# Gate matmuls in pairs on 64-row tiles, squares side by side, and their sum ahead of gates 0 and 1 on VectorE

## What is computed

```python
x = x + window_attention(_ln_c(x))        # 8x8 windows, 4 heads of 16, relative bias, projection
t = _to_tokens(x)                         # 65,536 tokens of 64 channels
u = _ln_t(t)                              # over a token's 64 channels
probs = softmax(u @ router_w + router_b)  # 8 experts
top_p, top_i = top_k(probs, 2); top_p /= sum(top_p)
t = t + sum_k top_p[k] * (u @ expert_w[top_i[k]] + expert_b[top_i[k]])
```

## Time and profile before

| | |
|---|---|
| median of 3 runs | 1270.95 us |
| lowest, highest | 1270.83, 1271.89 us |
| profiled execution, its own time | 1268.81 us |
| its span, first to last instruction | 1267.0 us |
| granted TensorE clock, mean | 0.983 |
| TensorE matmuls busy | 1192.4 us, 94% |
| GpSimd busy | 1081.7 us, 85% |
| VectorE busy | 1053.9 us, 83% |
| ScalarE busy | 920.4 us, 73% |

### The profile page before, as it was taken

One profiled execution on the slowest core, in us unless ns is written; L12 is line 12 of the kernel. 1 busy time (PEld: TensorE's weight loads), 2 busy tenths in 40 slices (PEclk: granted clock), 3 DMA queues, 4 the chain that ended last, 5 costly groups with the idle time before them and its releaser, 6 DMA issues.

```text
span 1267.0 us, 47630 instructions
## 1 busy us (share of the span) xinstructions
PE 1192.4 (94%) x19840; PEld 729.4 (58%) x19840; DVE 1053.9 (83%) x2247; ACT 920.4 (73%) x1743; POOL 1081.7 (85%) x925
## 2 busy tenths in 40 slices
PE   4579999999999999999999999999999999999986
PEld 3456666655565666656566666655556565666531
DVE  6458898888888889898888888988888888888874
ACT  6368778867777887877677888777767776777742
POOL 6368999989888999999988899998988888888753
PEclk9599999999999999999999999999999999999998
DMA  7012333322223233322222333332222222222221
GB/s 203 5 38 66 92 94 86 81 61 71 55 60 81 77 90 94 91 59 61 70 55 62 95 88 86 88 87 55 58 65 66 53 65 65 63 56 66 64 70 42
DMA packets 95622, 91.43 MB, mean 72 GB/s; under 512 B 26928, under 2 KB 62384, under 8 KB 95408
## 3 DMA queue, kind: packets, MB, share of 16 engines
q1 hardware_dynamic: 95408, 88.37, 27.6%
HBM read 35.90 MB, written 17.83 MB: 42 GB/s over the span
## 4 chain that ended last, share of the span: by engine, by line
PE 67%; DVE 10%; POOL 7%; DMA 7%; issue 5%; ACT 5%; SPq 0%; DVEq 0%; POOLq 0%; ACTq 0%
PE bank_y L530 16%; PE bank_s L410 8%; PE bank_t L425 8%; PE bank_s L384 6%; PE bank_o L464 4%; PE bank_g L518 4%; DMA r_b<-recip_rows 4%; PE bank_o L438 4%; PE bank_p L454 4%; PE bank_p L518 3%; DVE t_g L992 3%; DMA recip_rows<-r_out 2%; PE bank_t L394 2%; PE bank_y L502 2%; DVE prob L880 2%
## 5 line engine op out<-in xcount | busy, mean ns | idle before, releaser
L1142 POOL TENSOR_TENSOR t_g<-t_t,g_copy 128x512 f32<-128x512 f32 x192 | 245.6, 1292 | 72.0 <-ACT g_copy L712 70.8
L530 PE MATMUL bank_y<-t_g,w_exp 128*64 128x512 f32 x1024 | 268.9, 616 | 6.7 <-DVE t_g L992 4.7
L1120 POOL TENSOR_TENSOR prob<-prob,mx 128x512 f32<-128x512 f32 x256 | 261.8, 1045 | 14.7 <-DVE mx L887 14.5
L675 ACT ACTIVATE prob<-prob 128x512 f32<-128x512 f32 x256 | 159.4, 623 | 128.6 <-POOL prob L1120 128.6
L992 DVE TENSOR_TENSOR t_g<-t_t,bank_p 128x512 f32<-128x512 f32 x256 | 174.2, 680 | 9.2 <-PE bank_p L518 7.3
L880 DVE TENSOR_TENSOR prob<-bank_s,rel 128x1024 f32<-128x1024 f32 x128 | 156.3, 1221 | 28.4 <-PE bank_s L410 23.7
L425 PE MATMUL bank_t<-idn,prob 128*128 128x128 f32 x1024 | 163.6, 283 | 5.5 <-ACT v_bd L670 5.0
L679 ACT ACTIVATE prob_t<-bank_t 128x512 f32<-128x512 f32 x256 | 152.5, 596 | 21.3 <-PE bank_t L425 21.2
L712 ACT ACTIVATE g_copy<-bank_g 128x512 f32<-128x512 f32 x192 | 113.8, 593 | 74.1 <-PE bank_g L518 73.9
L425 PEld LDWEIGHTS bank_t<-idn,prob 128*128 128x128 f32 x1024 | 112.8, 141 | 79.2 <-issue 65.9
L887 DVE TENSOR_REDUCE mx<-prob 128x16 f32<-128x1024 f32 x128 | 155.4, 1214 | 2.2
(11 more groups left out here) (122 smaller groups left out, 2345.1 us busy)
## 6 DMA issues: line engine op xcount, KB each, us to landing
t_t<-t_rout SPq DMA_DIRECT2D x256, 128.0 KB, 2.4
x_in<-in_x SPq DMA_DIRECT2D x68, 256.0 KB, 3.3
r_b<-recip_rows SPq DMA_DIRECT2D x64, 256.0 KB
out_y<-y_out SPq DMA_DIRECT2D x128, 128.0 KB, 2.6
r_in<-sum_b SPq DMA_DIRECT2D x64, 16.0 KB
recip_rows<-r_out SPq DMA_DIRECT2D x64, 16.0 KB, 1.7
t_g<-in_sel SPq DMA_DIRECT2D x1, 512.0 KB, 3.6
rel<-in_relb SPq DMA_DIRECT2D x1, 256.0 KB, 2.9
```

The source lines that it names most:

```text
L530: mm(B_Y[C * a:C * a + C, :], w_exp[:, pair, :], t_g[:, (2 * pair + a) % TG, :], start=False, stop=(pair == MIXES // 2 - 1), skip_group_ch ...
L675: A(prob[:, i], prob[:, i], ACT.Exp).then_inc(p_ready.sem, 1)
L1120: G.tensor_tensor(sc, sc, mx[:, i, :].unsqueeze(2).broadcast_to([P, 2 * HEADS, NTOK]), ALU.subtract).then_inc(s_shifted.sem, 1)
L1142: G.tensor_tensor(t_g[:, u % TG, :], t_t[:, p, u % 2, :], g_copy[:, n, :], ALU.mult).then_inc(tg_pool.sem, 1)
```

## The change

The gates' parts go to other groups of `g3`, so that the first four groups (rows 0 to 63) hold all three parts for even gate matmuls, and the last four (rows 64 to 127) for odd ones. Each gate matmul then uses its 64 rows alone. Gate matmul 2 goes behind the turned logits, next to 3, and 5 goes from behind the fourth turn of probabilities to ahead of it, next to 6. Gate matmuls 4 and 7 stay where they are. The bias matmul still uses all 128 rows, with its parts in another order. `x_sq` is laid out with the eight planes of a column side by side; the squares' write steps over 32 bytes, the sum's read is contiguous. The sum is issued ahead of products 0 and 1.

```diff
--- before.py
+++ after.py
@@ -52,8 +52,9 @@
 SQUARES, PLANES, SCALES = range(3)
 CHUNK = 32
 PARTS = 3
-GATE_PARTS = (0, 0, 0, 1, 1, 1, 2, 2)
-BIAS_PARTS = (0, 1, 2, 0, 1, 2, 0, 1)
+GATE_PARTS = (0, 1, 2, 0, 1, 2, 0, 1)
+BIAS_PARTS = (0, 0, 0, 1, 1, 1, 2, 2)
+SEL_PARTS = ((0, 1, 2), (4, 5, 6))
 STAGES = ("project", "attend", "output", "route", "mix")
 LN_C_EPS, LN_T_EPS = 1e-6, 1e-5
 
@@ -110,7 +111,7 @@
 
         x_in = sb("x_in", [P, RING, 4, W])
         xt = sb("xt", [P, 2 * C, H])
-        x_sq = sb("x_sq", [P, 2, 4, H])
+        x_sq = sb("x_sq", [P, H, 2 * 4])
         plane_sum = sb("plane_sum", [P, 4, H])
         sums2 = sb("sums2", [P, H, GROUPS // 2])
         st = sb("st", [P, 5, H])
@@ -152,7 +153,7 @@
         g_copy = sb("g_copy", [P, len(ON_POOL), BANK])
         y_out = sb("y_out", [P, 4, W])
 
-        FIRST_SQ = (x_sq, prob[:, 0:2].rearrange("p i h n k -> p (i h n k)").rearrange("p (m c h) -> p m c h", m=2, c=4))
+        FIRST_SQ = (x_sq, prob[:, 0:2].rearrange("p i h n k -> p (i h n k)").rearrange("p (h x) -> p h x", x=2 * 4))
         B_S = ctx.enter_context(nc.psum_tensor("bank_s", [P, 2, BANK], F32))
         B_T, B_O, B_E, B_P, B_G, B_Y = (
             ctx.enter_context(nc.psum_tensor(f"bank_{n}", [P, BANK], F32)) for n in "toepgy")
@@ -515,7 +516,8 @@
                     pe.wait_ge(g_copied.sem, g_copied.at(g, ON_POOL.index(u - 2) + 1))
                 elif u:
                     pe.wait_ge(tg_dve.sem, tg_dve.at(g, ON_DVE.index(u - 2) + 1))
-                mm(B_GATE[u % 2][:, :], gate_sel16[:, u, :], g_t[:, :], start=True, stop=True
+                rows = slice(C * (u % 2), C * (u % 2) + C)
+                mm(B_GATE[u % 2][:, :], gate_sel16[rows, u, :], g_t[rows, :], start=True, stop=True
                    ).then_inc(gate_done[u % 2].sem, 1)
 
             def experts(g, pair):
@@ -561,11 +563,10 @@
                     logits(j - 2)
                 if attending and work.take:
                     turn_probs(j, 1, work)
-                if mixing:
-                    gates(j - 3, 2)
                 if routing_on:
                     turn_logits(j - 2)
                 if mixing:
+                    gates(j - 3, 2)
                     gates(j - 3, 3)
                 if projecting:
                     project(j + 1, QUERIES)
@@ -581,12 +582,10 @@
                     take(work.batch, *work.take, 1, j)
                 if mixing:
                     experts(j - 3, 1)
-                if mixing:
                     gates(j - 3, 6)
+                    gates(j - 3, 5)
                 if attending:
                     turn_probs(j, 3, work)
-                if mixing:
-                    gates(j - 3, 5)
                 if outputting:
                     project_out(j - 1)
                 if projecting:
@@ -625,7 +624,8 @@
                 act.wait_ge(xt_ready.sem, xt_ready.at(n, 2 * r + m + 1))
                 act.wait_ge(sq_sums.sem, sq_sums.at(batch, max(t * 2 + r - (batch == 0), 0)))
                 act.sem_inc(passed, 1)
-                A(dst[:, m], xt[:, bass.ds(plane + (2 * r + m) * 4, 4), :], ACT.Square).then_inc(sq_ready.sem, 1)
+                A(dst[:, :, 4 * m:4 * m + 4].rearrange("p h c -> p c h"), xt[:, bass.ds(plane + (2 * r + m) * 4, 4), :],
+                  ACT.Square).then_inc(sq_ready.sem, 1)
 
             def first_take(batch, t, r):
                 for m in range(2):
@@ -817,7 +817,7 @@
                 pair = bass.ds(t * 2 + r, 1)
                 dve.wait_ge(sq_ready.sem, sq_ready.at(n, 2 * r + 2))
                 V.tensor_reduce(sums2[:, :, pair].rearrange("p h o -> p (h o)"),
-                                src[:, :, :, :].rearrange("p m c h -> p h (m c)"), AX.X,
+                                src[:, :, :], AX.X,
                                 ALU.add).then_inc(sq_sums.sem, 1)
 
             def first_sums(batch, t, r):
@@ -976,13 +976,13 @@
                     elif step == 15:
                         V.tensor_tensor(gates, hot, over_experts(share), ALU.mult).then_inc(route.sem, 1)
                     elif step == 16:
-                        V.tensor_copy(g3[:, :, 0:3, :], thrice(by_pair[0], 3)).then_inc(route.sem, 1)
+                        V.tensor_copy(g3[:, :, 0::3, :], thrice(by_pair[0], 3)).then_inc(route.sem, 1)
                     elif step == 17:
                         V.tensor_tensor(by_pair[1], by_pair[0], g3[:, :, 0, :], ALU.subtract).then_inc(route.sem, 1)
                     elif step == 18:
-                        V.tensor_copy(g3[:, :, 3:6, :], thrice(by_pair[1], 3)).then_inc(route.sem, 1)
+                        V.tensor_copy(g3[:, :, 1::3, :], thrice(by_pair[1], 3)).then_inc(route.sem, 1)
                     elif step == 19:
-                        V.tensor_tensor(g3[:, :, 6:8, :], thrice(by_pair[1], 2), thrice(g3[:, :, 3, :], 2), ALU.subtract).then_inc(route.sem, 1)
+                        V.tensor_tensor(g3[:, :, 2::3, :], thrice(by_pair[1], 2), thrice(g3[:, :, 1, :], 2), ALU.subtract).then_inc(route.sem, 1)
 
             def gate(g, p, u):
                 dve.wait_ge(gate_done[u % 2].sem, gate_done[u % 2].at(g, u // 2 + 1))
@@ -1011,11 +1011,11 @@
                     total_planes(work.batch)
                 if work.step == SCALES:
                     turn_root(work.batch)
+                if work.sums:
+                    sum_squares(work.batch, *work.sums)
                 if mixing:
                     gate(j - 3, 1 - p, 0)
                     gate(j - 3, 1 - p, 1)
-                if work.sums:
-                    sum_squares(work.batch, *work.sums)
                 if routing_on:
                     routing(j - 2, 1, 8)
                 if mixing:
@@ -1220,7 +1220,7 @@
     for g in range(2):
         bexp[:, g, :, g, :] = a["eb"]
         for e in range(EXPERTS):
-            sel[[0, 3, 6], g, e, e // 2 * 2 + g, e % 2, :] = 1.0
+            sel[list(SEL_PARTS[g]), g, e, e // 2 * 2 + g, e % 2, :] = 1.0
     kmask = np.zeros((2, HEADS, DH, 2), f)
     kbias = np.zeros((2, HEADS, DH, 2), f)
     for h in range(HEADS):
```

## The result

Five runs of each on one chip: **1280.54 us** for the changed kernel (1278.73 to 1282.67), 1270.95 for the one before (1270.2 to 1272.45). Ratio **1.0074**, 95% interval 1.006 to 1.0089: slower, by 9.6 us. The profiled execution took 1280.54 us, its span is 1278.8 (1267.0 before), its mean granted clock 0.973 (0.983).

The account below looks back on a forecast made before the run. Slots were taken as a front part tied to ScalarE and VectorE and a rear part of pure TensorE. Slot terms summed to +5.6 us on 1268.8, so 1274.4, plus 2.1 to the median: 1276.5 us, range 1256 to 1283.

Parts of the forecast that it names:

- the forecast case: Whole kernel: slot terms total +5.6 us, giving 1276.5 us; chance 0.52, its own range 1272 to 1283.
- Pairs overlap in full: Paired 64-row gate matmuls on TensorE: both run together and cost one 0.21 us; bounds 0 to 0.21 saved per pair.
- A change of shape costs 0.095: TensorE, between matmuls of different tile shape: 0.095 us each, five more a slot, 0.48 in all; bounds 0 and 0.10.
- Ordinary slots, +0.20: Slots without a take: each 0.20 us longer, so +5.0 over 25 ordinary and +1.8 over 9 with statistics.
- The -0.07 of the pair 6/5: Gates 6 and 5 with the turn between, up to the output's projection: from 0.97 to 0.90 us, saving 0.07.
- Take slots, 0: 21 slots with take and sums: gate and pair terms and the removed 0.11 us wait of experts 1 total 0.
- Sums alone, -0.51: 3 slots with sums but no take: +0.20 less the 0.71 us wait of experts 1, -1.5 us in all.
- The squares' write, taken as 0: ScalarE's stepped square write costs 0, idle time being behind both squares; up to +4.6 us in the first phase.
- the bound of 0.38 each: Upper bound for a stepped square write of 512 numbers on ScalarE: 0.38 us, from VectorE's 0.76 for 1024.
- rival 3: Every pair counts in full on TensorE: 3 x 0.21 x 64 = 41 us saved, 1230 us; chance 0.02.
- changes of rows alone: Rival 1: TensorE tile changes in rows alone are nearly free, -14.8 us together, 1256 us; chance 0.27.
- the pairs don't fail to overlap: Denies rival 2: pairs of gate matmuls do not overlap, +19 us on top, 1295 us; chance 0.06.

Follow-up runs that it names:

- the experiment: Changed kernel with gate matmuls 4 and 7 on all 128 rows, the three pairs left on 64: 1270.88 us, ratio 1.0 to the kernel before.
- the sums alone: Kernel before with only the new x_sq layout, stepped square write and sum ahead of products 0 and 1: 1273.43 us, ratio 1.0023.
- the gates alone: Changed kernel with the squares' layout and the sum's place as before, only the gates' part kept: 1279.99 us, ratio 1.0076 to the kernel before.

## Why the prediction was right, and where it was not

The sign and the forecast case held: the mechanism of the slots, 0.10 us for each change of shape against pairs that save little where they stand, is what the runs show. The size was 5.6 us forecast and 9.6 measured, within the range.

That it came this near is partly luck. All 5.6 us were forecast for the slots. The 61 slots with a forecast of their own became 4.8 longer, but only since misses cancel: 3.4 less than forecast in the ordinary and the statistics slots, 1.5 more with take and sums, 0.3 more with a take alone, 0.9 more with sums alone. Another 3.4 us ahead of the first mix and 3.6 at the end were not in the sum at all.

- **Pairs overlap in full.** Starts 0 to 0.05 us apart, as forecast, from the experts' and scores' float32 rows. With the same rows they come 0.23 apart.
- **A change of shape costs 0.095.** Held. The changed slot shows +0.10 ahead of the queries' projection, +0.09 at gate 4, +0.11 at gate 7; 0.21 for two in the experiment. No load stands ahead of gate 0: its load starts at 1162.42 and its matmul at 1162.43. The Trainium skill (TensorEngine Tiling (Array Packing), Key Properties) says that a change of the tiling mode drains the engine. The trace agrees in what it can show, also where only the rows change: the next load starts no earlier than its matmul, and 0.10 us are lost.
- **Ordinary slots, +0.20.** An undisturbed one became 0.24 longer: the terms at the queries' projection and at gate 7 came out one and two hundredths larger, and 0.01 is in none of the steps. The -0.07 of the pair 6/5 came out exactly. What failed is the multiplication by 25 and by 9: the slots of the two kinds together became 3.4 us longer and not 6.8, as the table of slots shows.
- **Take slots, 0.** Most became 0.04 to 0.06 longer, with the wait of 0.11 gone as forecast; with two longer ones this is +1.5 us over 21.
- **Sums alone, -0.51.** The wait of 0.71 went, but the three slots became shorter by 0.2 on average (18.72 to 18.52). "What is late next is TensorE itself" failed: with the sums alone it was once the reciprocals' transfer.
- **The squares' write, taken as 0.** This is the step that failed. The reason given was ScalarE's idle time within the pipeline. That held beside the pairs, which cover the slower copies, and not with the sums alone, where the turn of probabilities waits 0.26; and the bound of 0.38 each was itself too low, measured 0.53. In the first phase nothing hides it: +2.7 us, seen with the change and with the sums alone, and gone with the old squares. The Trainium skill (SBUF — State Buffer, section Door 1: The DMA port swizzle) has it that an access which moves on to a new 16-byte line pays; the traces agree for ScalarE's write, 632 against 1160 ns, and for its read, 1136. VectorE's price of a step, (1977 - 1214) / 1024 = 0.75 ns a number, did not carry over to ScalarE: (1160 - 632) / 512 = 1.03.
- **Nothing was set down for the end of the run.** See the last section: +3.8 us of the profile's span fell there, and what part of it belongs to the change is open.
- **Small slips in the working.** 3 x 0.21 is 0.63 and not 0.64, and rival 3's 3 x 0.21 x 64 is 40 us and not 41. Neither moves the forecast.

Of the rivals, changes of rows alone are not free, and the pairs don't fail to overlap. That each pair counts in full is out by the waits named: the logits for the token copy, gate 3 for product 1.

## What to carry to other kernels

Price a change of tile shape from two starts in your own trace, and count the entries a new tile makes on both its sides before you count what two tiles side by side save: here a pair is worth 0.21 us and each new neighbour of another shape costs 0.10, so a pair between two new neighbours is about even, it paid clearly only where a change stood already, and a single matmul on half the rows only lost. Such a gain counts where TensorE sets the pace; ahead of a wait for another engine it is lost. A layout that turns one engine's stepped read into another's stepped write moves the cost: look where the second engine has no cover, which here was the first phase. And check a forecast slot by slot: a total can come out near while its terms miss in both directions.

## What the runs showed that I had not expected

**ScalarE in steps.** 512 float32 numbers take 0.63 us with neighbours on both sides, 1.16 written in steps of 32 bytes, 1.14 read in steps of 512 bytes.

**A lower clock at the end.** In the last slots, which drain the pipeline, TensorE has less to do. Stretches there, of the changed kernel (columns as above; the clock is the third number from the end):

```profile
1245.00:1261.00 16.00, 11.45 (x45) 3.50 (x46) 8.34 (x25) 4.66 (x10) 6.54 (x5) 0.68 0.22 50
1261.00:1278.80 17.80, 10.18 (x35) 2.36 (x33) 5.05 (x11) 3.58 (x6) 3.82 (x3) 0.78 0.13 30
```

and of the kernel before:

```profile
1236.00:1252.00 16.00, 11.41 (x46) 3.69 (x46) 8.69 (x27) 4.97 (x11) 6.54 (x5) 0.79 0.22 50
1252.00:1267.00 15.00, 7.92 (x33) 2.19 (x33) 4.53 (x9) 3.06 (x6) 3.86 (x3) 0.96 0.15 36
```

The granted clock lies between the engine's two levels, full (2.4 GHz) and half (1.2 GHz), so part of each stretch ran at half. At the lower level the experts' group lasts 1.97 us, at the full one 1.08.

The last four slots and what follows them are 1.6 + 2.2 = 3.8 us longer than before: 81.5 us against 77.8. The profiles of the gates alone and of the pairs on the same rows show a clock as low in the last slices of the page (tenths 8, 7); those with old squares in the first phase, or with gates 4 and 7 on 128 rows, show 9, 7 and 9, 8, and the kernel before 9, 8. Two of the versions have the very instructions of the changed kernel over this stretch, since no squares are taken there. With old squares in the first phase it takes 78.6 us, with squares read in steps 79.9. So the same instructions over this stretch can differ by 2.9 us from one profiled execution to another, of the 3.8 in question. The gates alone take 81.7. Each kernel has one profiled execution, so it stays open whether the change makes the long end more frequent.
